# Block 0 and block 1's first products interleaved, five blocks of W2 turned by VectorE, and the sine tables moved in ScalarE's order

## The chip, the cores and the metric

The kernel runs on one core of one Trainium2 chip. The metric is the device time of one execution in microseconds (us). TensorE multiplies, VectorE, ScalarE and GpSimd work elementwise, and SyncE (SP) and ScalarE issue DMAs. In the profile they are PE (PEld its weight loads), DVE, ACT, POOL and SP.

## What is computed

Five steps on x (64 batches, 64 heads, 1024 positions): a masked causal convolution by a state-space kernel, added to x, then three linear layers. Cut to what matters here:

```python
x = x + L0(x, lengths, ...)                  # kernel K = 2 Re(C_s exp(dt*A*l)), convolved by FFT in the reference
# L1: top-2 of 8 language experts
y = x @ W1.T + 2 * sum_e gate_e * (x @ A_lang[e].T) @ B_lang[e].T
# L2: one of 5 labelers per batch
y = y @ W2.T + 0.5 * (y @ A_lab[label]) @ B_lab.T
# L3: weights quantized to a codebook of 64 codes, with scale per group of 128
delta = B3 @ A3 * 0.5
w = quantize((W3 + delta) / exp(scale)) * exp(scale) + delta
y = y @ w.T
```

The residual additions around the linear layers are in the kernel as identity matrices, added on the diagonals of W1, W2 and the quantized W3.

## The kernel before, in words

**Two stages.** The first 340 us fold the three linear layers into one matrix M; the rest applies it to 32 tiles of x, with the convolution. The change touches the first stage alone (the kernel's `order` and what hangs on it). All matrices are 1024 x 1024, in 8 blocks of 128 rows.

**The chain of the first stage.** `QT[kt] = (W2 + I)[kt] (W1 + I)`, for kt = 0 to 7. For it, W2 has to stand transposed in `A2`. W2 comes in blocks of 128 rows into two buffers (`W2s`); TensorE transposes a block in 8 pieces into two staging banks (`w2t(ot, half)`), and ScalarE copies each bank to `A2` (`take`). GpSimd then adds the identity to the block's diagonal (`a2_diagonal`, semaphore `a2_ready`), and to W1's blocks as they land (`e1_diagonal`, `e1_ready`). A product `qt(kt, part)` has 4 parts: two halves of the first 512 columns, the next 512, and the 128 low-rank columns. Block 0 runs as `qt0`, all 16 of its matmuls behind `e1_ready`. A full fp32 matmul is two instructions in the trace.

**The quantization** goes in quarters of 256 rows of W3 (q = 0 to 3). TensorE makes `delta(q, n)` (4 products of 2), ScalarE copies them. VectorE makes `vq = (W3 + delta) / scale` (`v_ready`), goes through the codebook's steps (chunks of TENSOR_SCALAR and TENSOR_TENSOR inside branches, L1585 and L1590), and adds the four steps that ScalarE compares for it (`compare(q, n)`, tile `above`, L1143 and L1677). The result is transposed by TensorE (`a3(q, n)`, 4 pairs a quarter, L903), copied by ScalarE to `A3`, and GpSimd adds the diagonal with pair q of quarter q (`a3_ready`, L617). The products `m(q, mt)`, mt = 0 to 9 (L942), multiply it by QT. The first one of a quarter waits for the fourth pair and the diagonal:

```python
if mt == 0:
    pe.wait_ge(stage_free, jobno[("a3", q, 3)] + 1)
    pe.wait_ge(a3_ready, QT_TILES * (q + 1))
```

ScalarE splits each m product in a high part and a copy, from which GpSimd makes the low part (L630).

**The tables of the convolution** need sines and exponentials: VectorE makes angles behind quarter 3, ScalarE runs `sines(0)`, `exponentials()` and `sines(1)` between its copies (three ACTIVATEs for one half of the tables, L1092 to L1094), and VectorE makes powers.

**The order** is written by hand: one list `order` of jobs, which TensorE, ScalarE and GpSimd each go through in order, doing their share of each job. Staging banks 0 and 1 alternate by job number: a job waits until ScalarE has taken the job two before it (`several`). SP issues all loads from one queue, in program order, with waits in it (`next_w2`, `next_w3`): W1, W2's block 1, B3, A3, quarter 0 of W3, and so on.

Of the kernel before, what the change touches and what calls it, by code (L numbers as in the profile page):

```python
# [32 lines left out]
P = 128  # L33
# [7 lines left out]
def resid_stack_kernel(nc, x, lengths, languages, labels, codebook, log_dt, C_ri, log_A_real, A_imag, D_skip,  # L41
# [193 lines left out]
    with ExitStack() as ctx:  # L235
# [22 lines left out]
        v_ready, above_done = sem("v_ready"), sem("above_done")  # L258
# [9 lines left out]

        def deltas(q):
            return [("delta", q, n) for n in range(2 * QT_TILES)]  # L270

        order = [("w2t", 0, 0), ("w2t", 0, 1), ("scale",), ("qt0", 0), ("codesT",), ("qt0", 1), ("codes",), ("w2t", 1, 0), ("w2t", 1, 1)]
        order += [("qt", 1, 0), ("b3t", 0), ("b3t", 1), ("qt", 1, 1)] + deltas(0) + [("w2t", 2, 0), ("w2t", 2, 1), ("qt", 1, 2)]
        order += [("at", 0), ("at", 1), ("wrt",)]
        between = {2: deltas(1)[:2], 3: deltas(1)[2:], 5: [("nat4",)] + deltas(2)[:2], 6: deltas(2)[2:]}
        for kt in range(2, NC):
            order += [("qt", kt, 0), ("qt", kt, 1)]  # L280
            if kt == 2:
                order += [("qt", 0, 3), ("qt", 1, 3)]
            if kt + 1 < NC:
                order += [("w2t", kt + 1, 0), ("w2t", kt + 1, 1)]
            order += between.get(kt, []) + [("qt", kt, 2), ("qt", kt, 3)]
# [73 lines left out]
        with nc.Block() as block:  # L359

            @block.sync
            def _(sp):
# [18 lines left out]
                def load_w2(ot):  # L381
                    sp.dma_start(W2s[:, ot % 2, :], W2[ot * P:(ot + 1) * P, :]).then_inc(ld_w2[ot % 2], 16)
# [7 lines left out]
                for it in range(NC):  # L390
                    sp.dma_start(E1[:, it, 0:L], W1[it * P:(it + 1) * P, :]).then_inc(ld_w1[it], 16)
                load_w2(1)
                sp.dma_start(B3n[:, :, :], B3_lora.rearrange("(t p) r -> p t r", p=P)).then_inc(ld_b3, 16)
                sp.dma_start(A3raw[:, :], A3_lora).then_inc(ld_a3, 16)
                for t in range(QT_TILES):
                    load_w3(0, t)

                def next_w2(ot):
                    sp.wait_ge(stage_full, jobno[("w2t", ot - 2, 1)] + 1)
# [9 lines left out]
                next_w2(3)  # L409
                sp.wait_ge(consts_ready, 1)  # L410
# [11 lines left out]
                for ot in range(4, NC):  # L422
                    next_w2(ot)
                    if ot == 5:
                        next_w3(1)
# [39 lines left out]
            def _(pool):  # L465
# [73 lines left out]
                def a2_diagonal(it):  # L539
                    pool.wait_ge(stage_free, jobno[("w2t", it, it // 4)] + 1)  # L540
# [12 lines left out]
                e1_diagonal(1)  # L553
                pool.wait_ge(e1_ready, 2)
# [4 lines left out]
                step(pool.tensor_scalar(t[2], t[1], MAGIC, None, ALU.subtract))  # L559
                e1_diagonal(2)  # L560
                pool.wait_ge(e1_ready, 3)
                madd(t[3], t[2], -LN2_HI, t[0])
                madd(t[4], t[2], -LN2_LO, t[3])
                e1_diagonal(3)
                pool.wait_ge(e1_ready, 4)
                step(pool.tensor_scalar(t[5], t[4], 1.0 / math.factorial(7), None, ALU.mult))
                poly(6)
                e1_diagonal(4)
                pool.wait_ge(e1_ready, 5)
                poly(5)  # L570
                poly(4)
                e1_diagonal(5)
                pool.wait_ge(e1_ready, 6)
                poly(3)
                poly(2)
                e1_diagonal(6)
                pool.wait_ge(e1_ready, 7)
                poly(1)
                step(pool.tensor_scalar(t[5], t[5], 1.0, None, ALU.add))
                e1_diagonal(7)  # L580
                pool.wait_ge(e1_ready, 8)
# [3 lines left out]
                step(pool.tensor_scalar(dtA_re, exps[:, 1:1 + N], dt, -1.0, ALU.mult, ALU.mult))  # L585
                step(pool.tensor_scalar(dtA_im, nat[:, 0, :], dt, None, ALU.mult))
                step(pool.tensor_scalar(turn_n, dtA_im, 1.0 / (2 * math.pi), MAGIC, ALU.mult, ALU.add))
                step(pool.tensor_scalar(turn_n, turn_n, MAGIC, None, ALU.subtract))
# [1209 lines left out]
```

## Time and profile before

| what | us |
|---|---|
| runs: median (lowest to highest) of 3 | 1013.91 (1013.37 to 1016.0) |
| the profiled execution | 1015.38 |
| its span, first to last instruction | 1013.5 |
| TensorE busy in the span | 994.4 |
| VectorE busy | 823.2 |
| ScalarE busy | 454.1 |
| GpSimd busy | 285.6 |

The profile is of one execution; times in it count from the span's start. The rows further down are from its page (shares, groups) and from its trace: a timeline has a row for each merged group of instructions of an engine, with the idle time before it in brackets and what ended that; a table of windows has the granted clock of TensorE as a share of full speed. The mean granted clock of the span was 0.998.

### The profile page before, as it was taken

How to read it: one execution, taken by the hardware profiler on the slowest of the kernel's cores; microseconds unless marked ns; L12 is line 12 of the kernel's file. 1: busy time of each engine (PE TensorE's matmuls, PEld its weight loads, DVE VectorE, ACT ScalarE, POOL GpSimd, SP SyncE). 2: the span in 40 equal slices, each digit the busy share in tenths (PEclk: the TensorE clock that was granted, in tenths of full speed). 3: DMA queues.
4: the chain of work that ended last, by engine and by line, in shares of the span. 5: the costliest groups of instructions: out<-in, count | busy, mean ns of one | idle time of the engine just before them, and what ended most of it. 6: DMA issues, size and time to landing. Idle time of an engine off the chain costs nothing.

```text
span 1013.5 us, 16370 instructions
## 1 busy us (share of the span) xinstructions
PE 994.4 (98%) x4767; PEld 799.7 (79%) x4767; DVE 823.2 (81%) x1617; ACT 454.1 (45%) x867; POOL 285.6 (28%) x343
## 2 busy tenths in 40 slices
PE   6999999999999999999999999999999999999997
PEld 3455558888888878888888888888888888888886
DVE  5499897989855688888888888888888888888863
ACT  1352523552367354534544355443544445454431
POOL 6300100644444422232222322233222332223200
PEclk9999999999999999999999999999999999999999
DMA  8602010100202444454445545455454544545321
GB/s 293 123 22 77 7 42 1 42 1 1 42 1 46 73 81 86 84 104 82 85 80 92 101 77 90 76 104 93 74 91 77 104 89 78 88 81 104 64 41 42
DMA packets 314676, 74.44 MB, mean 73 GB/s; under 512 B 290434, under 2 KB 307138, under 8 KB 314642
## 3 DMA queue, kind: packets, MB, share of 16 engines
q1 hardware_dynamic: 313634, 73.28, 37.6%
q10 hardware_dynamic: 1008, 0.76, 0.3%
q8 instruction: 15, 0.25, 0.1%
q14 instruction: 19, 0.16, 0.1%
HBM read 57.08 MB, written 16.91 MB: 73 GB/s over the span
## 4 chain that ended last, share of the span: by engine, by line
PE 95%; ACT 2%; DVE 1%; issue 1%; ACTq 1%; DMA 0%; SPq 0%; DVEq 0%
PE bank L719 34%; PE bank L942 13%; PE bank L884 11%; PE bank L709 10%; PE bank L740 4%; PE bank L689 4%; PE bank L700 4%; PE bank L678 4%; PE bank L895 2%; PE bank L864 2%; PE bank L746 1%; PE bank L730 1%; PE bank L824 1%; PE bank L903 1%; PE bank L667 1%
## 5 line engine op out<-in xcount | busy, mean ns | idle before, releaser
L719 PE MATMUL bank<-Mh,strips_r 128*128 128x512 f32 x1020 | 289.1, 395 | 0.0
L719 PEld LDWEIGHTS bank<-Mh,strips_r 128*128 128x128 f32 x1020 | 189.8, 188 | 41.1
L1015 ACT ACTIVATE SK<-ZZ 64x448 f32<-64x448 f32 x128 | 73.8, 577 | 214.9 <-DVE ZZ L1352 212.6
L719 PE MATMUL bank<-Ml,strips_r 128*128 128x512 f32 x510 | 160.0, 395 | 0.0
L501 POOL TENSOR_TENSOR Cl<-QC,Ch 128x256 fp32r<-128x256 f32 x32 | 24.1, 755 | 445.5 <-ACT Ch L997 445.5
L1352 DVE SCALAR_TENSOR_TENSOR ZZ<-ZZ,coef 128x192 f32<-128x192 f32 (+1 forms) x256 | 116.5, 495 | 10.1 <-DVE ZZ L1343 0.3
L719 PEld LDWEIGHTS bank<-Ml,strips_r 128*128 128x128 f32 x510 | 95.9, 188 | 22.5
L884 PE MATMUL bank<-E,A 128*128 128x512 f32 (+1 forms) x352 | 112.1, 477 | 0.8 <-ACT A L1085 0.8
L709 PE MATMUL bank<-Mh,strips_r 128*128 128x296 f32 x512 | 110.8, 300 | 0.3 <-DVE strips_r L1371 0.3
L884 PEld LDWEIGHTS bank<-E,A 128*128 128x128 f32 x352 | 56.8, 191 | 51.6 <-issue 50.2
L709 PEld LDWEIGHTS bank<-Mh,strips_r 128*128 128x128 f32 x512 | 85.0, 188 | 6.9 <-DVE strips_r L1371 6.3
L1343 DVE SCALAR_TENSOR_TENSOR ZZ<-ZZ,coef 128x384 f32<-128x384 f32 (+1 forms) x128 | 80.8, 631 | 7.0 <-issue 1.0
L709 PE MATMUL bank<-Ml,strips_r 128*128 128x296 f32 x256 | 76.8, 300 | 0.0
L1006 ACT ACTIVATE ZZ<-bank 64x448 f32<-64x448 f32 x128 | 68.5, 535 | 2.6 <-PE bank L678 0.3
L942 PE MATMUL bank<-A3b,QT 128*128 128x256 f32 x288 | 66.1, 388 | 0.0
L1323 DVE TENSOR_TENSOR strips_r<-strips,strips_r 128x512 fp32r<-128x512 f32 x64 | 61.5, 963 | 4.2 <-ACT strips_r L985 4.2
L942 PE MATMUL bank<-A3a,QT 128*128 128x256 f32 x288 | 63.5, 379 | 0.0
L630 POOL TENSOR_TENSOR Ml<-m,Mh 128x256 fp32r<-128x256 f32 x32 | 45.1, 1414 | 57.9 <-ACT m L1245 57.6
L942 PEld LDWEIGHTS bank<-A3b,QT 128*128 128x128 f32 x288 | 55.0, 194 | 7.9 <-issue 0.2
L942 PEld LDWEIGHTS bank<-A3a,QT 128*128 128x128 f32 x288 | 54.3, 190 | 7.2
L1028 ACT ACTIVATE strips_r<-strips 128x512 fp32r<-128x512 f32 x64 | 40.3, 632 | 37.6 <-DVE strips L1365 37.6
L689 PE MATMUL bank<-strips_r,toep 128*128 128x512 f32 x192 | 52.6, 409 | 0.6 <-DMA toep<-kpad 0.6
(303 smaller groups left out, 1794.5 us busy)
## 6 DMA issues: line engine op xcount, KB each, us to landing
X<-in_x SPq DMA_DIRECT2D x256, 64.0 KB, 2.8
XT<-in_x SPq DMA_DIRECT2D x256, 64.0 KB, 2.6
out_x<-O SPq DMA_DIRECT2D x62, 256.0 KB, 3.2
toep<-kpad SPq DMA_DIRECT2D x128, 64.0 KB, 2.2
E<-in_L_cond_W SPq DMA_DIRECT2D x8, 512.0 KB, 9.2
vq<-in_L_cond_weight SPq DMA_DIRECT2D x8, 512.0 KB, 3.6
W2s<-in_L_cond_W SPq DMA_DIRECT2D x7, 512.0 KB, 4.5
LA<-in_L_cond_lora_A SPq DMA_DIRECT2D x8, 80.0 KB, 3.6
```

Of the source, the lines that this page charges most:

```text
L630: pool.tensor_tensor(lo, m32[rows, n % 2, :], hi.bitcast(F32), ALU.subtract).then_inc(m_lo, 1)
L678: last = pe.matmul(psZ[hh][:, 0:SB].rearrange("p (c b) -> p c b", b=B), (Bh, Bl)[w][:, hh, :], (xh, xl)[p][:, 0:NC - 1, hh * B:(hh + 1) * ...
L689: last = pe.matmul(psY[hh][:, :].rearrange("p (c b) -> p c b", b=B), toep[:, hh, w, :], (xh, xl)[p][:, :, hh * B:(hh + 1) * B], start=(n = ...
L709: last = pe.matmul(psL[:, 0:LOWC], xs[:, c, :], ms[:, c, L:MW], start=(c == 0 and n == 0), stop=False, skip_group_check=True)
L719: pe.matmul(psO[nh][:, :], xs[:, c, :], ms[:, c, nh * BANK:(nh + 1) * BANK], start=(c == 0 and n == 0), stop=False)
L884: last = pe.matmul(bank[2 + 3 * (kt % 2) + n][:, 0:b - a], A2[:, it, kt * P:(kt + 1) * P], E1[:, it, a:b], start=(it == 0), stop=(it == NC ...
L942: last = pe.matmul(m_bank(n)[0:rows, 0:QO], lhs, A3[q % 2][:, kt, :], start=(kt == 0), stop=(kt == NC - 1))
L1006: act.activation(ZZ[hh * N:(hh + 1) * N, :, ri, :], psZ[hh][ri * N:(ri + 1) * N, 0:SB].rearrange("p (c b) -> p c b", b=B), ACT.Copy).then_ ...
L1015: act.activation(SK[ri * N:(ri + 1) * N, hh, :].rearrange("p (c b) -> p c b", b=B), ZZ[hh * N:(hh + 1) * N, :, ri, :], ACT.Copy).then_inc( ...
L1323: dve.tensor_tensor(xl[:, :, cols], xq[:, :, cols], xh[:, :, cols].bitcast(F32), ALU.subtract).then_inc(xl_done, 1)
L1343: dve.scalar_tensor_tensor(ZZ[:, dst, :, :], ZZ[:, src, :, :], coef[:, bass.ds(i, 1), power, 0], ZZ[:, dst, :, :], ALU.mult, ALU.add).then ...
L1352: dve.scalar_tensor_tensor(ZZ[:, dst, to, :], ZZ[:, src, of, :], coef[:, bass.ds(i, 1), power, n], ZZ[:, dst, to, :], ALU.mult, ALU.add).t ...
```

## The change

Four parts.

1. **Block 0 and block 1 side by side.** The 32 matmuls of `qt0` and the first 32 of block 1 alternate by W1's block (`first_two`). Block 1's transposes come after the first pair, and the codebook's, B3's and quarter 0's jobs stand between. SP loads W2's block 1 ahead of W1's block 1, and B3 and A3 ahead of W1's blocks 3 to 7. GpSimd adds W1's diagonals later between its small steps, and W2's block 1 diagonal earlier.
2. **W2 from block 3 on by VectorE.** The `w2t` jobs of blocks 3 to 7 are gone from TensorE and ScalarE. SP loads such a block in 4 DMAs, rearranged in pieces of 32 elements, so that a transpose of 32x32 blocks gives the whole transpose. VectorE does it by one instruction to each block (`w2_turn`): blocks 3, 4 and 5 in quarter 0 (before the last branch, behind the compared steps, at its end), blocks 6 and 7 in quarter 1 (behind `v_ready`, ahead of the compared steps).
3. **VectorE's order.** The exponential of the decays goes from quarter 0's end to the time before the quarter; B3's low parts go ahead of the codes' steps.
4. **ScalarE's order.** `sines(0)` goes from behind m(2, 4) to behind m(2, 5), `sines(1)` from behind a3(3, 3) to behind m(2, 8), and the comparisons 0 and 1 of quarter 0 to behind block 1's products. The A_lang and Wr transposes go behind half of block 2's products.

The core of the diff:

```diff
-        order = [("w2t", 0, 0), ("w2t", 0, 1), ("scale",), ("qt0", 0), ("codesT",), ("qt0", 1), ("codes",), ("w2t", 1, 0), ("w2t", 1, 1)]
-        order += [("qt", 1, 0), ("b3t", 0), ("b3t", 1), ("qt", 1, 1)] + deltas(0) + [("w2t", 2, 0), ("w2t", 2, 1), ("qt", 1, 2)]
-        order += [("at", 0), ("at", 1), ("wrt",)]
+        def first_two(*its):
+            return [("qt0", kt, it) for it in its for kt in range(2)]
+
+        order = [("w2t", 0, 0), ("w2t", 0, 1), ("scale",), ("qt0", 0, 0), ("w2t", 1, 0), ("w2t", 1, 1), ("qt0", 0, 1), ("qt0", 1, 0),
+                 ("qt0", 1, 1), ("codesT",)] + first_two(2) + [("b3t", 0), ("b3t", 1)] + first_two(3) + [("codes",)] + first_two(4)
+        order += deltas(0) + first_two(5, 6) + [("w2t", 2, 0), ("w2t", 2, 1)] + first_two(7)
...
-                order += [("qt", 0, 3), ("qt", 1, 3)]
-            if kt + 1 < NC:
-                order += [("w2t", kt + 1, 0), ("w2t", kt + 1, 1)]
+                order += [("at", 0), ("at", 1), ("wrt",), ("qt", 0, 3), ("qt", 1, 3)]
...
+                    for k in range(PARTS):
+                        sp.dma_start(W2s[k * SPAN:(k + 1) * SPAN, ot % 2, :].rearrange("p (c a r) -> p c a r", c=NC, a=PARTS),
+                                     bass.AP(W2.tensor, ot * P * L + k * SPAN,
+                                             [[L, SPAN], [P, NC], [SPAN * L, PARTS], [1, SPAN]])).then_inc(ld_w2[ot % 2], 16)
...
+                load_w1(0)
                 load_w2(1)
+                load_w1(1)
+                load_w1(2)
                 sp.dma_start(B3n[:, :, :], B3_lora.rearrange("(t p) r -> p t r", p=P)).then_inc(ld_b3, 16)
                 sp.dma_start(A3raw[:, :], A3_lora).then_inc(ld_a3, 16)
+                for it in range(3, NC):
+                    load_w1(it)
...
+                def w2_turn(ot):
+
+                    dve.wait_ge(ld_w2[ot % 2], 16 * ((ot % 2 == 0) + 1 + PARTS * ((ot - W2_BY_PE) // 2 + 1)))
+                    dve.transpose(A2[:, :, ot * P:(ot + 1) * P].rearrange("p t (a j) -> p t a j", a=PARTS),
+                                  W2s[:, ot % 2, :].rearrange("p (t a r) -> p t a r", t=NC, a=PARTS)).then_inc(w2_turned, 1)
...
-                        if (q, n) == (LAST_Q, 3):
-                            sines(1)
...
-                        if j == ("m", 2, 4):
+                        if j == ("m", 2, 5):
                             sines(0)
                         elif j == ("m", 2, 6):
                             exponentials()
+                        elif j == ("m", 2, 8):
+                            sines(1)
```

TensorE's queue at the program's start, before (ident with W2s is a block's transposes, E with A the first-stage products, cbw, tau, cb and codesT the codebook, B3n the low-rank factor):

```order
L829 MATMUL bank<-ident,W2s 128x128 x8
L803 MATMUL bank<-ident,scale_97 128x8 x8
L864 MATMUL bank<-E_86,A_87 128x512 x8
L835 MATMUL bank<-ident,cbw 64x128
L835 MATMUL bank<-ident,tau 64x128
L835 MATMUL bank<-ident,cb 64x128
L864 MATMUL bank<-E_86,A_87 128x512 x8
L840 MATMUL bank<-sel,codesT 128x64 x2
L829 MATMUL bank<-ident,W2s 128x128 x8
L884 MATMUL bank<-E_86,A_87 128x512 x4
L809 MATMUL bank<-ident,B3n 64x128 x8
L884 MATMUL bank<-E_86,A_87 128x512 x4
```

The same place in the changed kernel:

```order
L855 MATMUL bank<-ident,W2s 128x128 x8
L829 MATMUL bank<-ident,scale_97 128x8 x8
L889 MATMUL bank<-E_86,A_87 128x512 x2
L855 MATMUL bank<-ident,W2s 128x128 x8
L889 MATMUL bank<-E_86,A_87 128x512 x6
L861 MATMUL bank<-ident,cbw 64x128
L861 MATMUL bank<-ident,tau 64x128
L861 MATMUL bank<-ident,cb 64x128
L889 MATMUL bank<-E_86,A_87 128x512 x4
L835 MATMUL bank<-ident,B3n 64x128 x8
L889 MATMUL bank<-E_86,A_87 128x512 x4
L866 MATMUL bank<-sel,codesT 128x64 x2
```

Block 1's transposes moved from behind sixteen products to behind two, and each small job now has products on both sides.

ScalarE's queue around m(2, 8), before (R1h is the high part of m(2, 8), m its copy, the A3b under it the copy of the fourth transposed pair of quarter 3, theta, rem and turns the sines, R2s m(2, 9)):

```order
L1238 ACTIVATE R1h<-bank 128x256
L1245 ACTIVATE m_94<-bank 128x256
L1085 ACTIVATE A3b<-bank 128x512
L1092 ACT_TABLE_LOAD
L1092 ACTIVATE theta<-rem 128x1344
L1093 ACTIVATE rem<-rem 128x1344
L1094 ACTIVATE turns<-rem,half_pi 128x1344
L1238 ACTIVATE R2s<-bank 96x256
```

The same place in the changed kernel:

```order
L1264 ACTIVATE R1h<-bank 128x256
L1271 ACTIVATE m_94<-bank 128x256
L1119 ACT_TABLE_LOAD
L1119 ACTIVATE theta<-rem 128x1344
L1120 ACTIVATE rem<-rem 128x1344
L1121 ACTIVATE turns<-rem,half_pi 128x1344
L1112 ACTIVATE A3b<-bank 128x512
L1264 ACTIVATE R2s<-bank 96x256
```

The table load and the three sine instructions moved from behind the copy of the fourth pair to ahead of it.

## Rows read from the trace of the kernel before

**Rows 1.** The page, busy time of each engine: us, share, instructions.

```profile
PE 994.4 (98%) x4767; PEld 799.7 (79%) x4767; DVE 823.2 (81%) x1617; ACT 454.1 (45%) x867; POOL 285.6 (28%) x343
```

**Rows 2.** Timeline of TensorE, start: start us, us, instruction, count, idle before.

```profile
10.72 10.12 PE L864 MATMUL bank<-E,A 128*128 128x512 f32 x16
...
21.01 7.03 PE L864 MATMUL bank<-E,A 128*128 128x512 f32 x16
27.97 0.66 PE L840 MATMUL bank<-sel,codesT 64*128 64x64 f32 x4
...
30.82 3.67 PE L884 MATMUL bank<-E,A 128*128 128x512 f32 x8 [0.78 <-ACT A L1085]
```

**Rows 3.** The same timeline, transposes of blocks 4, 5 and 6 of W2.

```profile
80.06 1.04 PE L829 MATMUL bank<-ident,W2s 128*128 128x128 f32 x8
81.35 0.50 PE L824 MATMUL bank<-A3hh,B3s 128*128 128x512 f32 x1 [0.25 <-ACT A L1085]
...
97.92 1.04 PE L829 MATMUL bank<-ident,W2s 128*128 128x128 f32 x8
98.79 15.69 PE L884 MATMUL bank<-E,A 128*128 128x512 f32 x48
114.31 1.04 PE L829 MATMUL bank<-ident,W2s 128*128 128x128 f32 x8
115.69 0.43 PE L845 MATMUL bank<-ident,nat 64*128 64x64 f32 x4 [0.34 <-ACT A L1085]
```

**Rows 4.** Timeline of VectorE: quarter 0, the decays' exponential, quarter 2, a transpose.

```profile
41.84 2.62 DVE L1651 TENSOR_TENSOR vq<-vq,dq 128x1024 f32<-128x1024 f32 x2 [3.61 <-ACT dq L1085]
...
49.51 1.59 DVE L1585 TENSOR_SCALAR step_t<-vq,steps 128x1024 f32<-128x1024 f32 x2 [2.01 <-DVEq L1672]
...
66.10 1.53 DVE L1585 TENSOR_SCALAR step_t<-vq,steps 128x1024 f32<-128x1024 f32 x2 [1.57 <-DVEq L1672]
...
89.51 0.18 DVE L1480 TENSOR_SCALAR ex<-nat 64x64 f32<-64x64 f32 x1
...
92.83 0.22 DVE L1490 TENSOR_TENSOR nat<-ex,ex_bits 64x64 f32<-64x64 f32 x1
...
176.68 9.51 DVE L1677 SCALAR_TENSOR_TENSOR quant<-above,fixed_rise,quant 128x2048 f32<-128x2048 uint8 x4 [3.17 <-ACT above L1143]
...
303.54 1.30 DVE L1306 STREAM_TRANSPOSE strips<-X 128x512 f32<-128x512 f32 x2
```

**Rows 5.** Timelines of ScalarE and TensorE where quarter 1's products begin.

```profile
207.77 2.00 ACT L1143 ACTIVATE above<-vq,fixed_tau 128x2048 uint8<-128x2048 f32 x1 [5.12 <-DVE vq L1652]
...
218.41 0.67 ACT L1085 ACTIVATE A3b<-bank 128x512 f32<-128x512 f32 x1
...
220.37 13.98 PE L942 MATMUL bank<-A3b,QT 128*128 128x256 f32 x64
```

**Rows 6.** Timeline of SP's queue: issue of eight x tiles, 64 KB each.

```profile
253.40 4.06 SPq L331 DMA_DIRECT2D X<-in_x  x8
```

**Rows 7.** Timelines of ScalarE, GpSimd and TensorE where quarter 3's products begin; GpSimd at the start.

```profile
289.80 0.61 ACT L1085 ACTIVATE A3b<-bank 128x512 f32<-128x512 f32 x1
...
294.43 1.42 ACT L1094 ACTIVATE turns<-rem,half_pi 128x1344 f32<-128x1344 f32 x1
...
290.67 2.19 POOL L617 TENSOR_TENSOR A3b<-A3b,ident 128x128 f32<-128x128 f32 x2
...
292.96 17.55 PE L942 MATMUL bank<-A3b,QT 128*128 128x256 f32 x80
...
8.47 0.45 POOL L537 TENSOR_TENSOR E<-E,ident 128x128 f32<-128x128 f32 x1 [4.41 <-DMA E<-in_L_cond_W]
```

**Rows 8.** Window's granted clock (last but two column), and timeline of TensorE around it.

```profile
321.00:322.00 1.00, 1.00 (x3) 0.50 0.24 36
...
320.37 4.09 PE L942 MATMUL bank<-A3b,QT 128*128 128x256 f32 x10
...
359.53 0.44 PE L700 MATMUL bank<-Sh,Ch 128*128 128x448 f32 x1 [1.32 <-DVE strips_r L1358]
```

More of the change, by code:

```diff
@@ L420, in next_w3 @@
                         load_w3(q, t)
[L422 to L425, printed above, removed]
+                next_w2(5)
+                next_w2(6)
+                next_w3(1)
+                next_w2(7)
                 for q in range(2, QUARTERS):
@@ L854, in wrt, with qt0 @@
                     several(("wrt",), NC, lambda ps, c: pe.transpose(ps[:, c * E:(c + 1) * E], Wr_nat[:, c * P:(c + 1) * P], ident[0:E, 0:E]))
-                def qt0(part):
-                    if part == 0:
-                        pe.wait_ge(a2_ready, 1)
-                        pe.wait_ge(stage_free, jobno[("w2t", 0, 1)] + 1)
-                    for it in range(part * NC // 2, (part + 1) * NC // 2):
-                        pe.wait_ge(e1_ready, it + 1)
-                        for n in range(2):
-                            last = pe.matmul(bank[2 + n][:, :], A2[:, it, 0:P], E1[:, it, n * BANK:(n + 1) * BANK],
-                                             start=(it == 0), stop=(it == NC - 1))
-                    if part == 1:
+                def qt0(kt, it):
+                    if it == 0:
+                        pe.wait_ge(a2_ready, kt + 1)
+                        pe.wait_ge(stage_free, jobno[("w2t", kt, 1)] + 1)
+                    pe.wait_ge(e1_ready, it + 1)
+                    for n in range(2):
+                        last = pe.matmul(bank[2 + 3 * kt + n][:, :], A2[:, it, kt * P:(kt + 1) * P], E1[:, it, n * BANK:(n + 1) * BANK],
+                                         start=(it == 0), stop=(it == NC - 1))
+                    if it == NC - 1:
                         last.then_inc(qt_main, 1)
@@ L1184, in _ @@
                         take(j, AT[:, :, ER:ER + E], stage(j)[:, 0:NC * E].rearrange("p (c e) -> p c e", c=NC))
-                        compare(0, 0)
-                        compare(0, 1)
                     elif name == "qt0" or (name == "qt" and which[1] == 2):
-                        kt = 0 if name == "qt0" else which[0]
-                        if j == ("qt0", 0):
+                        kt = which[0]
+                        if name == "qt0" and which[1] < NC - 1:
                             continue
@@ L1552, in _ @@
                 dve.tensor_scalar(sel[:, :], iota[0:K_CODES, :], codesT[:, 0, 0:1], None, ALU.is_equal).then_inc(sel_ready, 1)
+                for g in range(2):
+                    cols = slice(g * BANK, (g + 1) * BANK)
+                    dve.wait_ge(b3_hi, g + 1)
+                    dve.scalar_tensor_tensor(B3s[R3:2 * R3, cols], bank[(4, 7)[g]][0:R3, :], 0.5, B3s[0:R3, cols].bitcast(F32),
+                                             ALU.mult, ALU.subtract).then_inc(b3_lo, 1)
+                dve.wait_ge(b3_hi, 3)
+                dve.tensor_tensor(A3lo[0:R3, :], A3raw[0:R3, :], A3hh[0:R3, :].bitcast(F32), ALU.subtract).then_inc(b3_lo, 1)
                 dve.wait_ge(stage_free, jobno[("codes",)] + 1)
@@ L1660, in _ @@
                         worth = 1 << bit
+                        if q == 0 and worth == 1:
+                            w2_turn(3)
                         with dve.If((n_kept & worth) > 0):
@@ L1674, in _ @@
                     n_step[0] = base + per * (K_CODES - 1)
+                    if q == 1:
+                        w2_turn(7)
                     for n in range(FIXED):
```

87 lines of the change are left out of this document (52 added, 35 removed).

## The prediction

> **What bounds the kernel now.** I read the page's engine shares first, then TensorE's timeline over the first 345 us, then the timelines of the engines it waits for. TensorE is busy 98% of the span [rows 1], so the reader should look for two things: work that leaves TensorE, and places where another engine finishes just as TensorE needs it. Three facts come out.
>
> First, at the start the products run at half rate. The first sixteen 512-column instructions take 10.12 us, the next sixteen 7.03 [rows 2]; the difference, about 3.2 us, is TensorE at the lower of its two levels (1.2 against 2.4 GHz) from 10.8 to about 16 us (the page's clock row doesn't show it, the durations do). No load of W1 is waited for. So "behind W1's loads" hides nothing.
>
> Second, the transposes of W2's blocks stand in TensorE's queue between products. Third, from the quantization on, ScalarE and GpSimd hand over tiles with margins of 0 to 1.3 us; the change moves ScalarE work at such a place.
>
> **The change part by part.** A profiled execution took 1015.38 us with a span of 1013.5; the median of the runs is 1013.91. The sum below is a difference inside the span, and I apply it to the median (for the profiled execution add 1.5).
>
> *Turns that leave TensorE.* Blocks 3 to 7: from the transposes' start to the next instruction's start 1.29 us (80.06 to 81.35), 0.87 (97.92 to 98.79), 1.38 (114.31 to 115.69) [rows 3]; blocks 3 and 7 repeat the first with 1.28 and 1.29. Sum -6.1 us. Bounds: 5 x 0.87 = 4.4 if the waits behind them came back in another form, 6.1 if not. I take 6.1: what follows is products or the delta pair, whose staging banks were freed long before.
>
> *Side by side at the start.* Codes and block 1's turns took 27.97 to 30.82, 2.85 us, for 0.6 + 0.87 us of work [rows 2, 3]; ScalarE's copies were waited for. In the new order products stand behind each of these, so 1.4 goes. Five brackets of 0.2 to 0.8 us like that one, up to 64 us, bring another 1.5 with their drain; the pair of deltas keeps its own. Together -2.9 (bounds -1.5 and -3.4). The half-rate stretch stays: same time, other work in it.
>
> So TensorE reaches the quantized quarters 9.0 us earlier, if the others keep up.
>
> *VectorE.* A stream transpose of 128x512 twice took 1.30 us [rows 4]; a turn is 128x1024, so 1.3 each (bounds 1.3 and, under GpSimd's traffic, 2.6). Two of the five (blocks 3 and 6) stand before branches; the engine idled 1.57 and 2.01 us there while it passed them [rows 4], so these cost nothing; three cost 3.9. The first quarter starts with the fourth delta, which comes 5.0 us earlier (41.84 to about 36.9). The exponential of the decays (89.51 to 93.05, 3.55 us) goes to a stretch where VectorE idled. The 3.17 us it waited for ScalarE's comparison at 176.68 [rows 4] vanish, as that comparison moves with TensorE. Net: VectorE 7.8 us earlier when it makes the last quarter's values. ScalarE stands at its comparison until then (207.77), and its backlog ends with the take at 218.41 + 0.67 = 219.08, 1.3 us ahead of the product at 220.37 [rows 5]. TensorE waits there by 9.0 - 7.8 - 1.3, less than nothing: 0 (bounds 0 and 2.5, if no turn hides in a branch).
>
> *When block 3 is ready.* The branch of turn 3 was reached at 64.5 (66.10 - 1.57) [rows 4], now 5.0 earlier; with its 1.3 the turn ends near 61 us. TensorE wants block 3 at 69 (73.4 less the 2.9 and one turn); block 4 at 77 against 85; the others have 9 us or more. GpSimd's diagonal (0.45 us [rows 7]) lies between, not more.
>
> *Loads.* W2's blocks now come in 128-byte pieces, 4 issues each. Eight x tiles of such pieces and the same 512 KB in sum were issued in 4.06 us [rows 6]; a block is wanted 20 us after its issue, so nothing. On SP the third to seventh block of W1 now stand behind the two low-rank loads (B3 and A3); even if they are issued only at 16 us, products on block 3 of W1 start at 26. LA, kpad and D wait behind block 4's load until 44 us; LA is read at 151, kpad's store is waited for at 67. GpSimd adds W1's diagonals between smaller steps: the fourth at 21.5, wanted at 26; the sixth and eighth also 5 us or more ahead. Each at zero.
>
> *Sines.* This is what the other terms don't pay for. In the last transposed quarter ScalarE took the fourth transpose pair at 289.80, and only then ran its second sines until 295.85. GpSimd added the diagonal from 290.67, took 2.19 us, ended at 292.86, and TensorE began the last quarter's products at 292.96 [rows 7]: margin nil. Now the sines stand ahead of that take. In the same frame: take at 289.80 + 5.4 = 295.2, done 295.8, diagonal 296.1 to 298.3, product at 298.4 instead of 292.96. TensorE stands idle: +5.4 us. The tables that the sines feed are wanted later than before, so nobody gains. Lower bound: two lone GpSimd adds of 0.45 [rows 7] instead of 2.19 give +4.1. The 2.19 lay beside VectorE's tensor-by-tensor products, and beside the sines' end there is one again, so I take 5.4. (The Trainium skill, GPSIMD Engine Reference, section 8, "Key points", says GpSimd's SBUF interfaces are contended by VectorE instructions with two SBUF inputs; by it the 2.19 stays, without it 1.3 us less. No run here separates them.)
>
> The first sines go one product later: the take of the second pair comes 4 us later, still ahead of the fourth pair that reuses its bank. Zero.
>
> *Clock after that wait.* The clock fell to 0.50 from about 320.8 to 324.2 us, after a stretch of 16-column instructions, and ten instructions took 4.09 us [rows 8] instead of 2.2 (17.55 / 80 each [rows 7]): a fall cost 1.9 at most. A gap of 1.32 us before 359.53 [rows 8] did not lower it. A gap of 5.4 us lies on the far side of both; I take one such fall: +1.7 (bounds 0 and 3.2, the loss at the start).
>
> Sum: -6.1 - 2.9 + 0 + 5.4 + 1.7 = -1.9 us, 1012.0. What the two engines' gain was worth is mostly given back at one product.
>
> **The rivals.** *No fall of the clock:* everything as above without +1.7: 1010.3. For it: the one gap seen is harmless. Against: its length. (The Trainium skill, TensorE: Matmul & The Clock Gate, section "What's actually happening", has half rate as the default state that activity lifts and idleness brings back; by it 1012.0, without it 1010.3.)
>
> *No wait at the last quarter:* the gain arrives whole, 1013.9 - 9.0 = 1004.9, or near 1007.6 if half the wait is there. Only if the sines were short or the diagonal early; ScalarE's order speaks against it.
>
> *Late warm-up:* eight 128-column transposes now stand inside the half-rate stretch, where unbroken 512-column products stood when the clock rose at 16. If it rises once such a step later, +1.7: 1013.7.
>
> *VectorE becomes the bound (slower):* if the turns cost more or its start comes less early, ScalarE stands longer at the last comparison and TensorE waits at 220. The wait is 7.7 us minus VectorE's gain. Slower by over 3.04 us when that gain is below 2.8; with none, 7.7 + 5.4 + 1.7 - 9.0 gives 1019.7. For it: engines that share traffic are slow here, as GpSimd's two adds of 0.45 that took 2.19 [rows 7]. Against: GpSimd is nearly idle where the turns stand.
>
> That the block turned by VectorE isn't what the products need would show in the output, not in time; I give it no chance.
>
> **How the numbers follow.** Within 0.3% (3.04 us, about what a measurement of this kernel can tell from no change) is 1010.9 to 1017.0. Forecast 0.45, late warm-up 0.14: same, 0.59. No fall 0.20, no wait 0.13: faster, 0.33. VectorE 0.08: slower. The predicted time is the forecast's. The range runs from 1007.0, which takes in the nearer half of "no wait", to 1016.0, which takes in 2.5 us at 220 and most of a second loss of clock; left out are the rest of "no wait" and VectorE's case, under 2 in 10.
>
> **What would show it.** Right: the first 128x256 product of the last quarter starts after a TensorE idle of 4 to 5.5 us ended by GpSimd's diagonal; that product's first instructions at 0.50 clock; lap products starting at 151 to 152 instead of 160.67; no TensorE transposes of W2 after block 2; three of five VectorE transposes in the open. Wrong: no idle there; an idle before the 128x256 product at 211; lap products after 155, which would put the loss in the early stage (turned blocks or loads late).

## The result and the profile after

The changed kernel takes 1016.34 us (median of 20 runs, 1013.86 to 1018.88) against 1014.24 for the kernel before (20 runs beside them): ratio 1.0017, 95% interval [1.0009, 1.0025]. That is within 0.3%, but 4.3 us above the predicted 1012.0 and just past the top of the range, 1016.0. The profiled execution took 1016.38 us with a span of 1014.6 and a mean granted clock of 0.994 (before: 1013.5, 0.998).

The page, engine shares (TensorE lost 3.8 us of work, and the span is longer) and the row of the granted clock in 40 slices, which reads 9 everywhere in the page before and has one 8 here:

```profile
PE 990.6 (98%) x4727; PEld 798.6 (79%) x4727; DVE 828.6 (82%) x1622; ACT 449.0 (44%) x857; POOL 288.0 (28%) x343
...
PEclk9999999999989999999999999999999999999999
```

TensorE's timeline, columns as in [rows 2]; the rows at which the kernels can be laid side by side:

```profile
11.18 3.78 PE L889 MATMUL bank<-E,A 128*128 128x512 f32 x4
14.75 1.52 PE L855 MATMUL bank<-ident,W2s 128*128 128x128 f32 x8
16.11 5.32 PE L889 MATMUL bank<-E,A 128*128 128x512 f32 x12
...
151.58 2.41 PE L922 MATMUL bank<-LA,E 128*128 128x160 f32 x16 [0.38 <-ACT dq L1112]
...
281.06 3.62 PE L969 MATMUL bank<-A3a,Bw 128*96 128x256 f32 x16
290.72 19.93 PE L969 MATMUL bank<-A3b,QT 128*128 128x256 f32 x80 [6.04 <-issue]
...
320.49 2.40 PE L969 MATMUL bank<-A3b,QT 128*128 128x256 f32 x10
...
331.74 1.66 PE L715 MATMUL bank<-strips_r,toep 128*128 128x512 f32 x6 [1.33 <-DMA toep<-kpad]
...
358.75 0.44 PE L726 MATMUL bank<-Sh,Ch 128*128 128x448 f32 x1 [1.30 <-DVE strips_r L1386]
...
360.84 1.14 PE L766 MATMUL bank<-R1h,hgTh 128*128 128x512 f32 x2
```

The same instructions in the timeline of the kernel before, as far as the prediction's rows don't hold them:

```profile
160.67 2.41 PE L895 MATMUL bank<-LA,E 128*128 128x160 f32 x16 [0.37 <-ACT dq L1085]
...
289.49 3.62 PE L942 MATMUL bank<-A3a,Bw 128*96 128x256 f32 x16
...
310.35 0.38 PE L667 MATMUL bank<-ident,QB 128*128 128x128 f32 x2
...
332.56 1.66 PE L689 MATMUL bank<-strips_r,toep 128*128 128x512 f32 x6 [0.57 <-DMA toep<-kpad]
```

Side by side they are a ledger of the gain (m(1,0) starts at 211.83 in the changed kernel, the instruction behind the 80 at 310.49):

| place | before | after | earlier by |
|---|---|---|---|
| lap products | 160.67 | 151.58 | 9.09 |
| m(1,0) | 220.37 | 211.83 | 8.54 |
| m(2,9) | 289.49 | 281.06 | 8.43 |
| m(3,0), 80 instructions | 292.96 | 290.72 | 2.24 |
| the next, behind the 80 | 310.35 | 310.49 | -0.14 |
| toep, 6 instructions | 332.56 | 331.74 | 0.82 |
| end of the span | 1013.5 | 1014.6 | -1.1 |

All that was won by 281 us is gone by 310. (Behind that, toep is 0.8 us early again, because the profile of the kernel before has a fall of the clock between the two places and this one has none there; the fall at 360 us then takes it back.) The gain goes in two steps: 6.2 us of waiting ahead of m(3,0), and 2.4 us because its 80 instructions take 19.93 us instead of 17.55 [rows 7]. The first step, in the timelines of ScalarE (the table load and the sine instructions, then the take of the fourth pair) and GpSimd:

```profile
281.50 1.28 ACT L1119 ACT_TABLE_LOAD   x1
282.79 1.32 ACT L1119 ACTIVATE theta<-rem 128x1344 f32<-128x1344 f32 x1
...
285.50 1.41 ACT L1121 ACTIVATE turns<-rem,half_pi 128x1344 f32<-128x1344 f32 x1
286.83 0.58 ACT L1112 ACTIVATE A3b<-bank 128x512 f32<-128x512 f32 x1
...
287.48 3.14 POOL L643 TENSOR_TENSOR A3b<-A3b,ident 128x128 f32<-128x128 f32 x2 [4.18 <-ACT A3b L1112]
```

GpSimd's diagonal ends at 290.62, and m(3,0) begins at 290.72. The bracket of the product names "issue" as what ended its idle, so that the diagonal ended it is read from these two times and from the wait in the code.

The second step, in windows of 4 us (busy time of each engine, then the granted clock, third from the end of a row, before DMA share and GB/s):

```profile
288.00:292.00 4.00, 1.28 (x3) 1.13 (x4) 3.93 (x3) 0.00 (x0) 3.83 (x3) 0.60 0.00 0
292.00:296.00 4.00, 4.00 (x11) 3.18 (x11) 1.99 (x2) 0.00 (x0) 0.61 (x1) 0.55 0.00 0
296.00:300.00 4.00, 4.00 (x20) 3.52 (x20) 2.96 (x6) 0.66 (x2) 0.73 (x1) 1.00 0.13 21
360.00:364.00 4.00, 3.92 (x14) 3.01 (x13) 3.05 (x7) 0.69 (x2) 0.00 (x0) 0.57 0.18 28
```

The clock stands near its lower level (0.50 is 1.2 GHz) in the end of the idle and in the first 5 us of work, where 11 instructions fit in 4 us instead of 20. The last row is a second fall, which costs the pair of L766 1.14 us for 0.66. It comes 2 us behind an idle of 1.30 us (the row at 358.75), at the place where [rows 8] have the gap of 1.32 us that was not followed by a fall. Meanwhile the fall of before [rows 8] is missing here, its x10 take 2.40 instead of 4.09.

VectorE's turns took 1.25 us each. Three of the five:

```profile
60.81 1.25 DVE L1608 STREAM_TRANSPOSE A<-W2s 128x1024 f32<-128x1024 f32 x1 [0.76 <-DVEq L1713]
...
99.92 1.24 DVE L1608 STREAM_TRANSPOSE A<-W2s 128x1024 f32<-128x1024 f32 x1
101.99 1.54 DVE L1623 TENSOR_SCALAR step_t<-vq,steps 128x1024 f32<-128x1024 f32 x2 [0.83 <-DVEq L1713]
...
122.11 1.25 DVE L1608 STREAM_TRANSPOSE A<-W2s 128x1024 f32<-128x1024 f32 x1 [0.33 <-DVE quant L1628]
```

### The profile page after: what moved, and what is told of

It is laid out like the page before. It is cut to its first block, busy times and chain, and to the rows that moved or that the text cites. A ratio compares the mean times of both kernels' runs of the same rounds, so it can differ in the third digit from the quotient of the medians.

```text
span 1014.6 us, 16298 instructions
## 1 busy us (share of the span) xinstructions
PE 990.6 (98%) x4727; PEld 798.6 (79%) x4727; DVE 828.6 (82%) x1622; ACT 449.0 (44%) x857; POOL 288.0 (28%) x343
## 4 chain that ended last, share of the span: by engine, by line
PE 77%; DVE 11%; issue 6%; ACT 3%; DMA 1%; ACTq 1%; DVEq 1%; SPq 0%
PE bank L745 34%; PE bank L735 10%; PE bank L969 9%; PE bank L766 5%; PE bank L715 4%; PE bank L726 4%; PE bank L704 4%; DVE quant L1720 3%; PE bank L889 2%; DVE quant L1628 1%; PE bank L772 1%; DVE vq L1688 1%; DVE quant L1726 1%; PE bank L756 1%; DVE quant L1725 1%
## 5 line engine op out<-in xcount | busy, mean ns | idle before, releaser
L911 PE MATMUL bank<-E,A 128*128 128x512 f32 (+1 forms) x320 | 97.8, 466 | 0.0
L911 PEld LDWEIGHTS bank<-E,A 128*128 128x128 f32 x320 | 51.1, 191 | 44.8 <-issue 44.3
L656 POOL TENSOR_TENSOR Ml<-m,Mh 128x256 fp32r<-128x256 f32 x32 | 41.0, 1285 | 68.4 <-ACT m L1271 68.2
```

The lines of the kernel that those rows point to most:

```text
L656: pool.tensor_tensor(lo, m32[rows, n % 2, :], hi.bitcast(F32), ALU.subtract).then_inc(m_lo, 1)
L911: last = pe.matmul(bank[2 + 3 * (kt % 2) + n][:, 0:b - a], A2[:, it, kt * P:(kt + 1) * P], E1[:, it, a:b], start=(it == 0), stop=(it == NC ...
```

## The experiments

Theory: the second sines make the wait of 6.2 us, the wait makes a fall of the clock that costs 2.4 us or more, and without the sines the parts add up to a gain of 8 to 9 us. Rivals: the wait has another cause; the clock's falls come and go and have nothing to do with the wait; the turns or the new start give less than the ledger credits to them. Medians of the kernel before were 1014.24 beside the changed kernel, 1013.73 beside the first four runs, 1013.70 beside the next four and 1014.57 beside the last, so runs of different batches are compared by their ratios; 0.001 is 1.0 us.

### Both sines back

```diff
+                        if (q, n) == (LAST_Q, 3):
+                            sines(1)
...
-                        if j == ("m", 2, 5):
+                        if j == ("m", 2, 4):
...
-                        elif j == ("m", 2, 8):
-                            sines(1)
```

> The changed kernel with both sines back where they stood in the kernel before: the first behind m(2,4)'s take, the second behind the take of the last transpose pair a3(3,3). My theory: in the changed kernel 6.0 us of idle TensorE ahead of m(3,0) come from the second sines alone, and a fall of TensorE's granted clock (0.50 from 289 to 295 us) that costs 2.4 us comes from that idle. So m(3,0) should start near 284.5 (before 292.96, changed 290.72), its 80 products take 17.6 us again, and the time should be 1016.3 - 6.2 - 2.4 = 1007.7; down to 1005.8 if the later fall at 360 us goes as well. Rival 1, the wait is true but the clock falls somewhere in any case: 1010 to 1011. Rival 2, the wait was not the sines' (GpSimd's diagonal or the matrix itself is late whatever ScalarE does): idle ahead of m(3,0) stays, 1015 to 1017.

Measured: 1005.81 us, ratio 0.9924 [0.9912, 0.9936]. TensorE's timeline and GpSimd's:

```profile
280.83 3.62 PE L969 MATMUL bank<-A3a,Bw 128*96 128x256 f32 x16
284.31 17.55 PE L969 MATMUL bank<-A3b,QT 128*128 128x256 f32 x80
...
323.17 1.65 PE L715 MATMUL bank<-strips_r,toep 128*128 128x512 f32 x6 [1.53 <-DMA toep<-kpad]
```

```profile
282.01 2.19 POOL L643 TENSOR_TENSOR A3b<-A3b,ident 128x128 f32<-128x128 f32 x2
```

No idle, full rate, and the whole early gain but some 1 us arrives: the theory's lower value. It is also the version that beats both kernels: 7.7 us below the kernel before by its ratio, 9.4 below the changed one (0.9924 against 1.0017; 10.5 by the medians, which are of two batches). This profile has no fall, so it is best laid beside a profile of the kernel before without one (its second, below: lap products at 160.37, m(1,0) at 220.06, m(3,0) at 292.66, span 1012.2). The lap products (151.38 here) come 9.0 us earlier, m(1,0) (211.61) 8.45, m(3,0) 8.35, toep 7.9, and the end of the span 7.9: 0.5 us are lost ahead of m(1,0), as in the changed kernel, and 0.45 at toep, where the idle grows from 1.08 to 1.53 because the DMA came forward by less than TensorE. The row of the kernel before:

```profile
331.07 1.65 PE L689 MATMUL bank<-strips_r,toep 128*128 128x512 f32 x6 [1.08 <-DMA toep<-kpad]
```

### The second sines alone, on the kernel before

```diff
-                        if (q, n) == (LAST_Q, 3):
-                            sines(1)
...
+                        elif j == ("m", 2, 8):
+                            sines(1)
```

> The kernel before with one step moved: the second sines ahead of the take of a3(3,3), as in the changed kernel; turns and start as before. My theory: the same wait and the same fall as in the changed kernel, so slower than before by 5.4 to 6.2 us of idle and 1.7 to 2.4 us of clock: 1021 to 1023, with an idle ahead of m(3,0) of about 6 us that GpSimd's diagonal ends. Rival 1, the wait comes from the turns (VectorE or GpSimd late) and not from the sines: 1014 as before. Rival 2, the wait costs its idle alone, the clock's falls being there in both kernels: 1019.4 to 1020.2.

Measured: 1021.72 us, ratio 1.0088 [1.0073, 1.0103]. The timeline:

```profile
298.33 19.22 PE L942 MATMUL bank<-A3b,QT 128*128 128x256 f32 x80 [6.04 <-issue]
```

The same idle to the hundredth and 1.7 us on the 80 instructions, without any other part of the change. Moved alone, these four ScalarE instructions cost 8.9 us by the ratio.

### Work in the wait: the clock apart from the idle

```diff
+        FILL = 13
...
+                        if q == LAST_Q:
+                            pe.wait_ge(m_taken, mno[("m", 2, 8)] + 1)
+                            for _ in range(FILL):
+                                pe.matmul(bank[2][:, 0:QO], QT[:, 0, 0:P], A3[0][:, 0, :], start=True, stop=True)
```

> The changed kernel with thirteen products of 128x256 added on TensorE in the wait ahead of m(3,0), into a bank that the next product overwrites; nobody reads their results. They take about 5.6 us, less than the 6.0 of idle, so the wait stays and TensorE is merely not idle in it. My theory (the idle lowers the clock): the fall at 289 to 295 us is gone, the 80 products of m(3,0) take 17.6 instead of 19.9 us, the time is 2.4 us below the changed kernel, 1013.9; 1012.5 if the fall at 360 us was a consequence too. Rival 1, the clock falls there by its own rule whatever TensorE does in the wait: same as the changed kernel, 1016.3. Rival 2, the products run past the end of the wait or hold a bank: 1017 and above, with m(3,0) starting later than 290.7.

Measured: 1011.62 us, ratio 0.998 [0.997, 0.9991]. The timeline, and a window:

```profile
284.20 5.78 PE L961 MATMUL bank<-A3a,QT 128*128 128x256 f32 x26
290.41 17.50 PE L974 MATMUL bank<-A3b,QT 128*128 128x256 f32 x80 [0.43 <-issue]
```

```profile
288.00:292.00 4.00, 3.57 (x18) 2.83 (x17) 3.90 (x4) 0.00 (x0) 3.83 (x3) 1.00 0.00 0
```

m(3,0) starts within 0.3 us of where it did, so the wait is untouched; TensorE merely works in it, and the fall is gone. By the ratios (1.0017 to 0.998) that is worth 3.8 us, by the medians 4.7. The intervals of the two ratios leave about 1.3 us on either side (my estimate), so the value lies between 2.4, what one fall was expected to give, and 5.1. The other fall is not tied to the wait: this profile has one from about 357 to 360 us, again behind an idle of 1.31 us (355.31). With this run the 9.4 us that the sines cost are split: 5.7 of waiting (0.998 to 0.9924), 3.8 of clock, each give or take some 1.5 by the intervals (an estimate too).

### Half the work in the wait

```diff
-        FILL = 13
+        FILL = 6
```

> The changed kernel with six products (twelve instructions, 2.65 us) added in the wait ahead of m(3,0) instead of thirteen; nobody reads their results. The wait ends when it did, about 290.5; TensorE stands idle in its last 3.5 us, not in all 6.0. With everything else as in the changed kernel it tells how the clock answers to the length of the idle alone. My theory, 3.5 us is already enough: m(3,0)'s 80 products take 19 to 20 us, 1014 to 1016. Rival 1, it is not: 17.5 us for them, and the time of the run with thirteen products, 1011.6. Rival 2, the fall is there but shorter: between.

Measured: 1012.41 us, ratio 0.9988 [0.9979, 0.9997].

```profile
289.96 19.19 PE L974 MATMUL bank<-A3b,QT 128*128 128x256 f32 x80 [3.45 <-issue]
```

The profiled execution has the fall, with 1.6 us lost instead of 2.4, as the theory and the second rival said. Here the clock is granted in full until 291.0, 1 us after the products began, so all of the fall lies in work but it is short: it is over by 294.5. Three of the twelve executions had a mean clock of 1.000, so this idle does not lower it every time. The median is 0.8 us above that of the run with thirteen products and below the 1014 to 1016 that I expected; the intervals (0.9979 to 0.9997 and 0.997 to 0.9991) don't separate the two runs.

### Part of the second sines ahead of the take

```diff
                         elif j == ("m", 2, 8):
-                            sines(1)
+                            sines(1, range(1))
...
+                        if (q, n) == (LAST_Q, 3):
+                            sines(1, range(1, 3))
```

> The changed kernel with the second sines split: table load and the first of their three ScalarE instructions stay ahead of the take of a3(3,3), the other two (2.7 us) go behind it. The idle ahead of m(3,0) should be 6.0 - 2.7 = 3.3 us. It tells how the clock's loss goes with the length of the idle. My theory: an idle of 3.3 us still lowers the clock at the same place: 1016.3 - 2.7 = 1013.6. Rival 1, a gap of this length does not lower it (one of 1.3 us did not): 1016.3 - 2.7 - 2.4 = 1011.2. Rival 2, the clock's falls have nothing to do with the idle: fall rows at other places, and a time between the two.

Measured: 1008.9 us, ratio 0.9944 [0.9928, 0.996]. The idle was 1.11 us, not 3.3:

```profile
285.88 17.50 PE L969 MATMUL bank<-A3b,QT 128*128 128x256 f32 x80 [1.11 <-issue]
```

```profile
284.92 0.87 POOL L643 TENSOR_TENSOR A3b<-A3b,ident 128x128 f32<-128x128 f32 x2 [1.52 <-ACT A3b L1112]
```

Here GpSimd's two adds took 0.87 us instead of 3.14. VectorE's timeline points to the reason: in this run VectorE is idle beside them (284.81 to 287.60), in the changed kernel it works throughout, because the sines that it waits for are finished before the take and no longer behind it. So the run doesn't answer what it was made for, an idle of 3.3 us. Its one profile has a fall further on, at the place of [rows 8], behind the 16-column products:

```profile
313.22 4.09 PE L969 MATMUL bank<-A3b,QT 128*128 128x256 f32 x10
```

VectorE beside the adds:

```profile
282.84 1.97 DVE L1764 TENSOR_TENSOR theta<-theta,expo 128x1344 f32<-128x1344 f32 x1
287.60 1.56 DVE L1760 SCALAR_TENSOR_TENSOR rem<-theta 128x1344 f32<-128x1344 f32 x1 [2.79 <-ACT turns L1125]
```

```profile
287.02 1.56 DVE L1754 SCALAR_TENSOR_TENSOR rem<-theta 128x1344 f32<-128x1344 f32 x1 [2.31 <-ACT turns L1121]
288.62 1.69 DVE L1756 SCALAR_TENSOR_TENSOR rem<-rem,expo 128x1344 f32<-128x1344 f32 x1
290.34 1.69 DVE L1757 SCALAR_TENSOR_TENSOR theta<-theta,turns 128x1344 f32<-128x1344 f32 x1
```

(The first pair is this run, the three rows below it are the changed kernel.) With two of the three instructions ahead of the take:

```diff
-                            sines(1, range(1))
+                            sines(1, range(2))
...
-                            sines(1, range(1, 3))
+                            sines(1, range(2, 3))
```

> As the run with the split second sines, but two of the three ScalarE instructions (and the table load) ahead of the take of a3(3,3), one behind it. There the idle ahead of m(3,0) was only 1.11 us, since GpSimd's diagonal ran while VectorE stood idle and took 0.87 us instead of 3.14. Here the take comes 1.36 us later and VectorE is still idle, so m(3,0) should start at 285.88 + 1.36 = 287.2 with an idle of 2.5 us. My theory (short idles do not lower the clock, the one of 6.0 us does, and it is a loss in itself): 1005.8 + 1.4 = 1007.2 when no fall comes, up to 1009 as a median since a fall comes in some executions. Rival, 2.5 us lower the clock for certain: no run at a mean clock of 0.999 or 1.000, 1010 or more.

Measured: 1009.26 us, ratio 0.9961 [0.9947, 0.9975]; the diagonal again 0.87 us.

```profile
286.56 17.50 PE L969 MATMUL bank<-A3b,QT 128*128 128x256 f32 x80 [2.47 <-issue]
```

No fall at this place, and two of eight executions at 0.999 or more: the rival is out. The median is just past the top of what I expected, and falls aren't the whole reason: the profiled execution has none in its span and took 1008.81 us. My 1007.2 added 1.4 us to the time of the run with both sines back, but m(3,0) starts 2.25 us later than there (286.56 against 284.31), and the idle at toep is 2.06 us instead of 1.53. With these two it is 1008.6. Six of the eight executions have a mean clock of 0.998 or less; where it fell in them isn't shown.

### The turns alone, the new start alone

For the turns, the kernel before with the diff's `w2_turn`, `load_w2`, `a2_diagonal` and waits on `w2_turned`, and no more:

```diff
-            if kt + 1 < NC:
-                order += [("w2t", kt + 1, 0), ("w2t", kt + 1, 1)]
...
+                    if q == 0:
+                        w2_turn(4)
```

> The kernel before with VectorE's turns of W2's blocks 3 to 7 alone (their loads in 32-row pieces with them); the old start, the old place of the decays' exponential and the old sines. TensorE loses 6.1 us of transposes and should reach the lap products at 154.6. By the prediction's own formula VectorE starts no earlier, has three turns in the open (+3.9) and gets back the 3.17 us it waited for ScalarE, so its last values come 0.7 us later than before while TensorE comes 6.1 earlier: a wait of 6.1 + 0.7 - 1.3 = 5.5 us at m(1,0), whose clock then falls. That theory: 1013.7 - 6.1 + 5.5 = 1013.1 without a fall, 1015 to 1018 with one. Rival, the turns hide in VectorE's idle time: wait at m(1,0) below 1 us, 1007.6 to 1008.5.

Measured: 1014.11 us, ratio 1.0002 [0.9992, 1.0012]. The timelines of TensorE and ScalarE, and a window:

```profile
154.25 2.41 PE L911 MATMUL bank<-LA,E 128*128 128x160 f32 x16 [0.38 <-ACT dq L1101]
...
212.57 1.12 PE L919 MATMUL bank<-ident,quant 128*128 128x128 f32 x4 [2.35 <-ACT A3b L1101]
...
218.97 14.08 PE L958 MATMUL bank<-A3b,QT 128*128 128x256 f32 x64 [0.65 <-ACT A3b L1101]
```

```profile
207.59 2.00 ACT L1159 ACTIVATE above<-vq,fixed_tau 128x2048 uint8<-128x2048 f32 x1 [10.89 <-DVE vq L1674]
```

```profile
212.00:216.00 4.00, 3.43 (x11) 2.62 (x12) 4.00 (x5) 4.00 (x8) 3.41 (x4) 0.57 0.00 0
```

The lap products start 6.42 us earlier than before, m(1,0) only 1.40: 5.0 us are lost in between, in waits for ScalarE (2.35 and 0.65) and in a fall of the clock (0.50 from 213 to 216 us) that follows the first of them. None of the twelve executions had a mean clock above 0.998. ScalarE stands 10.89 us for VectorE's values, which come at 207.59, 0.2 us earlier than before [rows 5]. So the turns alone gain nothing: this is the mechanism of the prediction's rival on VectorE. The waits are shorter than my 5.5 us, since VectorE comes 0.2 us earlier and not 0.7 later (quarter 0 starts at 40.76, where it started at 41.84 before); the fall makes up for it (the x16 of m(0,9) took 4.84 us at L958 for 3.62, the four transposes 1.12 for 0.60).

The new start is the changed kernel with `W2_BY_PE = 8`, the transposes back in `order`, and both sines back:

```diff
-        W2_BY_PE = 3
+        W2_BY_PE = 8
...
+            if kt + 1 < NC:
+                order += [("w2t", kt + 1, 0), ("w2t", kt + 1, 1)]
```

> The changed kernel with all of W2's transposes on TensorE again and both sines in their old places: the two blocks' products side by side, the new order of W1's loads and of GpSimd's steps, and the decays' exponential in its new place remain. The prediction's term for it is -2.9 us (bounds -1.5 and -3.4): 1013.7 - 2.9 = 1010.8, with the lap products at 157.8 and no wait at m(1,0), as VectorE starts 5 us earlier and has no turns. Rival, that start gave more and the turns less than I said (the two together were right at 9.1): 1009 or below, or 1012 or above the other way.

Measured: 1011.73 us, ratio 0.9976 [0.9967, 0.9985]. Its lap products start at 158.25, 2.42 us earlier than before, and m(3,0) at 290.53, 2.43 earlier. By the ratios the two parts give 0 and 2.4 us when each stands alone, and 7.7 together: the new start brings VectorE forward, and only then is TensorE's saving of 6.4 us worth anything. Which part of the new start does it isn't separated: in the changed kernel its quarter 0 starts 5.1 us earlier (36.75 for 41.84), and the decays' exponential, 3.5 us of work, has left the chain behind it. No run has the one without the other.

### The first sines

Only the second sines back (the first diff above without its middle pair).

> The changed kernel with the second sines alone back behind the take of a3(3,3); the first sines stay one product later, as the change put them. The prediction priced that move at zero. My theory: like the run with both sines back, 1005.8 (1005 to 1007), m(3,0) at 284.3 without an idle. Rival, the first sines cost something too (their take of the second transpose pair comes 4 us later, and so does the exponential behind it): an idle at m(2,5) to m(2,8), 1007 or more.

Measured: 1006.71 us, ratio 0.9927 [0.9914, 0.9941], beside 0.9924 with both back. The times don't separate them; the profile shows a small price:

```profile
284.97 17.51 PE L969 MATMUL bank<-A3b,QT 128*128 128x256 f32 x80 [0.85 <-issue]
```

```profile
281.00 1.73 POOL L656 TENSOR_TENSOR R1l<-m,R1h 128x256 fp32r<-128x256 f32 x1 [0.27 <-ACT m L1273]
282.69 2.18 POOL L643 TENSOR_TENSOR A3b<-A3b,ident 128x128 f32<-128x128 f32 x2
```

GpSimd's step ahead of the diagonal took 1.73 us instead of 0.72 (289.99 in the timeline of before) and pushed it out by 0.7.

### Both kernels profiled again

No edit.

> The kernel before, unchanged, profiled once more: where its clock falls when it falls. My theory: the fall at 320.8 us in the first profile is one that comes in some executions only (of 31 runs 21 had a mean clock of 1.000), after the 16-column products or in the stretch from 352 to 364 us; with none the span is about 1011.7, with one 1013.4. Rival: it is always at the same place, and the span 1013.5 again.

> The changed kernel, unchanged, profiled once more. My theory: the fall at m(3,0) is there again (80 products in 19.2 to 20 us) because the idle of 6.0 us stands ahead of it; the second fall (360 us in the first profile) is one of those that come and go. Rival: the fall at m(3,0) is also one that comes and goes, and may be absent with the idle there.

Measured: before 1013.96 us, span 1012.2, mean clock 1.000, no fall anywhere in the span. Changed: 1017.0 us, span 1015.2, clock 0.993:

```profile
289.98 19.79 PE L969 MATMUL bank<-A3b,QT 128*128 128x256 f32 x80 [6.04 <-issue]
...
319.09 1.73 PE L941 MATMUL bank<-X1T,Vt 128*128 128x16 f32 x8
320.66 4.61 PE L969 MATMUL bank<-A3b,QT 128*128 128x256 f32 x10
```

The fall at m(3,0) is in both profiles of the changed kernel; the other one has moved from 360 to 319 us and is longer (4.61 us where full rate takes 2.40). Both theories' first halves hold.

### All executions together

The mean clock is listed for every execution, so falls can be counted without a profile, though not placed; the profile with a mean of 0.999 of the run with two sine instructions ahead has no fall in its span, hence the limit. Idle and the 80 instructions are from each kernel's profile:

| kernel | idle ahead of m(3,0) | its 80 instructions | executions at clock 0.999 or more |
|---|---|---|---|
| before (three series: 37 of 54) | 0 | 17.55 | 21 of 31 |
| both sines back | 0 | 17.55 | 5 of 6 |
| second sines back | 0.85 | 17.51 | 4 of 5 |
| new start alone | 0 | 17.56 | 10 of 12 |
| turns alone (idle 2.35 in quarter 1) | 0 | 17.55 | 0 of 12 |
| thirteen products in the wait | 0.43 | 17.50 | 5 of 8 |
| one sine instruction ahead | 1.11 | 17.50 | 2 of 6 |
| two ahead | 2.47 | 17.50 | 2 of 8 |
| six products in the wait | 3.45 | 19.19 | 3 of 12 |
| second sines alone | 6.04 | 19.22 | 0 of 6 |
| changed | 6.04 | 19.93 | 0 of 20 |

Of the changed kernel's 20 executions seven have a mean clock of 0.996 or 0.997 and spans of 1012.1 to 1013.1 us; the other thirteen have 0.991 to 0.995 and 1013.9 to 1017.1. The two profiles, both of the lower group, show the fall at m(3,0) and a further one; that the seven hold the first alone is read from their mean clock. The kernel before has one fall in one of its profiles and none in the other, and its median is an execution at 1.000.

## Why the prediction was wrong

By its own steps:

- **Turns off TensorE and the new start:** 9.0 us by the lap products was right together (9.09) and in its shares: -2.9 measured 2.4, -6.1 measured 6.4.
- **VectorE:** the net 7.8 us earlier was 7.3 (207.77 [rows 5] to 200.47). The turn of block 6 hid in front of its branch, that of block 3 but for 0.4 us (0.76 of idle and 1.25 of turn, for 1.57 of idle before), and 0.55 us was lost at m(1,0) where the sum had 0 with bounds 0 to 2.5. The rival's mechanism came true where the early start was taken away.
- **Loads and GpSimd at the start:** zero, and no late warm-up. The lower level cost 3.1 us before (10.12 less 7.03; the prediction's "about 3.2" is a misreading by 0.1), and 2.5 now (3.78 and 1.52 for 1.76 and 1.04): with the transposes inside the slow stretch, the product instructions from 16.11 on take 0.44 us each, where the four from 11.18 took 0.95.
- **The wait at m(3,0):** in its place, ended as said; 5.4 in the sum, 6.2 in the profile. The 0.8 is mostly GpSimd's diagonal, 3.14 us and not 2.19: I took the contention seen in [rows 7] as it stood, and the new place has more of it.
- **First sines:** 0 in the sum, about 0.7 us in one profile, too small for the times.
- **toep:** not in the sum. The DMA comes forward by less than TensorE. Against the 1.08 us of idle in the profile of before without a fall, 0.25 us more stay there in the changed kernel and 0.45 in the run with both sines back.
- **The clock is the step that failed.** "I take one such fall: +1.7 (bounds 0 and 3.2)" has the right mechanism and a wrong size, in two ways. The fall at m(3,0) costs 2.4 us in the profile, since the lower level lasts through 5 us of work, where that of [rows 8] lasted 3.4. And I priced one fall against a median that I took to hold the fall of the profiled execution, while most executions of the kernel before hold none, and most of the changed one hold a second. The run with the wait filled measured the term: 3.8 us by the ratios, where I had 1.7. With its noise (2.4 to 5.1) it is clear of the 1.7, but not of my upper bound of 3.2. The step's ground was thin as well: the gap of 1.32 us that "did not lower it" stood in one execution, and at the same place a gap of 1.30 is followed by a fall in the changed kernel; and an idle of 2.35 us, far below 5.4, is followed by one in the run of the turns alone.

By the runs' ratios the sum is -7.7 (everything but the sines) + 5.7 (wait) + 3.8 (clock), unrounded +1.7, where I had -9.0 + 5.4 + 1.7 = -1.9: 1.3 us from m(1,0), toep and the rest, 0.3 from the wait, 2.1 from the clock. In the medians the miss is 4.3, of which 0.3 is that the kernel before stood 0.3 us higher in the longer series (1014.24 for 1013.91). What isn't settled is why the second fall is more frequent behind the first: 13 of 20 executions of the changed kernel have one beyond the fall at m(3,0), while 10 of 31 of the kernel before have any. The run of the second sines alone has the same idle, and 2 of its 6 executions stand so low (0.993). No run separates a true link from a shifted timing.

## What to carry to other kernels

Work that is moved "behind other products" is in truth moved ahead of something in its own engine's queue. Find that instruction, and who waits for it with no margin; here four ScalarE instructions ahead of one copy turned a gain of 7.7 us into a loss of 1.7. Of parts that relieve different engines, the value is not a sum: relief of the busiest engine pays only if its suppliers come forward as well. And when a wait on TensorE opens, price the clock as well as the idle, and compare it with the runs' usual state, not with the one profiled execution.

## What the runs showed of the hardware

- The same two GpSimd adds (128x128 each) took 0.87 us beside an idle VectorE, 2.19 beside one tensor-by-tensor product followed by idle, and 3.14 beside VectorE's products without a pause. The slow ones end with VectorE's instructions: 0.73 us behind the end of the one product (290.02 + 2.11, adds done at 292.86), and 0.31 behind the end of the second of the two products that ran beside them (288.62 + 1.69, adds done at 290.62). So what they cost depends on where in VectorE's sequence they start. That there is such contention agrees with the Trainium skill, GPSIMD Engine Reference, section 8, "Key points": GpSimd's SBUF interfaces are contended by VectorE instructions with two SBUF inputs.
- In single profiles, idle times of 1.11 and 2.47 us ahead of m(3,0) left its 80 instructions at 17.50 us, and 3.45 us cost 1.6. An idle of 2.35 us ahead of quarter 1's transposes, in the run of the turns alone, was followed by a fall at once, and none of its 12 executions reached a mean clock of 0.999. With 3.45 us, 3 of 12 did; 6.04 us cost 1.7 to 2.4 in all three profiles, and no execution of 26 kept a mean clock of 0.999. The length of the idle alone doesn't tell whether the clock falls.
- Falls also come without such an idle, in about a third of the executions of the kernel before. In the profiles they stand at two places: behind the 16-column products (320.8 us before, 319 in the second profile of the changed kernel, 313 in the run with one sine instruction ahead), and about 2 us behind a gap of 1.3 us (360 in the changed kernel, 357 in the run with thirteen products). Other profiles pass both places at full clock.
